# A four-layer graph network on one core: a bias record of full height, another order of work where two graphs meet, and idle products in the ending

## What is computed

```python
# layer 0: convolution over the nodes, messages by distance, a GRU cell
h = relu(bn1(conv1d(x^T, w1, 1 tap)))
x_conv = relu(bn2(conv1d(h, w2, 17 taps)) + x^T)
s = x @ w_se.T + b_se                       # 3 factors per node
dist = sq[:, None] + sq[None, :] - 2 * s @ s.T      # sq = sum(s * s)
x_nmp = (exp(-dist) * mask) @ relu(x @ w_msg.T + b_msg)
r, z = sigmoid(...), sigmoid(...)           # gates of x, x_conv, x_nmp
n = tanh(gi_n + r * gh_n)
x0 = layernorm(x + (1 - z) * n + z * x)
# layer 1: attention on the edges, sigmoid(q @ k.T / sqrt(128)) * adj, normed by degree
# layer 2: logmap0, adj @ x, expmap0, project
# layer 3: adj + I normed by degree, a linear map, relu
```

## Time and profile before

| | |
|---|---|
| Time, median of 3 runs | 765.79 us (764.44 to 767.04) |
| The profiled execution | 766.93 us, span 765.1 us |
| TensorE products busy | 92% of the span |
| VectorE busy | 81% |
| ScalarE busy | 55% |
| GpSimd busy | 17% |
| TensorE's mean granted clock | 0.977 of full |

### The profile page before, as it was taken

One profiled execution on the slowest core, in us unless ns is written; L12 is line 12 of the kernel. 1 busy time (PEld: TensorE's weight loads), 2 busy tenths in 40 slices (PEclk: granted clock), 3 DMA queues, 4 the chain that ended last, 5 costly groups with the idle time before them and its releaser, 6 DMA issues.

```text
span 765.1 us, 12798 instructions
## 1 busy us (share of the span) xinstructions
PE 704.0 (92%) x3968; PEld 544.0 (71%) x3968; DVE 621.8 (81%) x2081; ACT 422.9 (55%) x883; POOL 131.3 (17%) x151
## 2 busy tenths in 40 slices
PE   4879999999999999999999999999999999998653
PEld 3666868777787877777786877778687777775541
DVE  7556788889888888889888888988888888976765
ACT  4353736657384655647374665738465564734351
POOL 0000111212121221212121121212122121211221
PEclk9999999999999999999999999999999999998787
DMA  5306041331605133250604233060513325101000
GB/s 203 124 7 226 17 152 69 124 126 28 220 15 178 55 132 115 77 170 14 211 36 151 82 123 124 23 224 14 178 55 127 120 71 176 56 12 59 0 15 28
DMA packets 46445, 75.26 MB, mean 98 GB/s; under 512 B 4050, under 2 KB 12628, under 8 KB 46292
## 3 DMA queue, kind: packets, MB, share of 16 engines
q1 hardware_dynamic: 46420, 74.96, 29.0%
HBM read 70.76 MB, written 4.19 MB: 98 GB/s over the span
## 4 chain that ended last, share of the span: by engine, by line
PE 62%; DVE 20%; ACT 8%; issue 6%; POOL 4%; DVEq 0%; ACTq 0%; POOLq 0%
PE C L1429 7%; PE F L1437 7%; PE K L1466 7%; PE K L1332 6%; PE F L1359 6%; PE K L1301 5%; PE CONV L1332 4%; PE C L1359 3%; PE C L1301 3%; POOL RSTD L367 3%; ACT X L427 2%; PE K L1320 2%; PE K L1475 2%; DVE X L717 2%; DVE Z L1032 2%
## 5 line engine op out<-in xcount | busy, mean ns | idle before, releaser
L348 POOL TENSOR_TENSOR RSTD<-VEPS,POW 128x4 f32<-128x4 f32 x48 | 49.2, 1024 | 293.1 <-DVE VEPS L711 293.1
L1332 PE MATMUL CONV<-H1H,WH 128*128 128x256 f32 x288 | 83.3, 289 | 2.9 <-DVE H1L L729 2.9
L1332 PE MATMUL CONV<-H1L,WH 128*128 128x256 f32 x288 | 81.9, 284 | 0.0
L1332 PE MATMUL CONV<-H1H,WL 128*128 128x256 f32 x288 | 81.5, 283 | 0.0
L1429 PE MATMUL C<-QT,KT 128*128 128x512 f32 x128 | 60.9, 616 | 4.1 <-DVE KT L869 3.4
L1301 PEld LDWEIGHTS K<-XS,BIG 128*128 128x128 f32 x496 | 59.4, 196 | 3.9 <-DVE XS L998 2.5
L1301 PE MATMUL K<-XS,BIG 128*128 128x128 f32 x496 | 59.8, 280 | 2.5 <-DVE XS L998 2.5
L1437 PE MATMUL F<-A,MSG 128*128 128x512 f32 x128 | 57.6, 593 | 1.1 <-issue 1.1
L1332 PEld LDWEIGHTS CONV<-H1H,WH 128*128 128x128 f32 x288 | 55.3, 192 | 4.5 <-ACT H L436 3.6
L1332 PEld LDWEIGHTS CONV<-H1L,WH 128*128 128x128 f32 x288 | 55.3, 192 | 0.7
L1332 PEld LDWEIGHTS CONV<-H1H,WL 128*128 128x128 f32 x288 | 55.5, 193 | 0.0
(11 more groups left out here) (273 smaller groups left out, 1946.2 us busy)
## 6 DMA issues: line engine op xcount, KB each, us to landing
ADJF<-in_adjT SPq DMA_DIRECT2D x16, 1024.0 KB, 5.3
ADJN<-in_adj SPq DMA_DIRECT2D x16, 1024.0 KB, 7.7
ADJM<-in_adjT SPq DMA_DIRECT2D x15, 1024.0 KB, 5.5
ADJR<-in_adjT SPq DMA_DIRECT2D x14, 1024.0 KB, 5.3
X_IN<-in_xT SPq DMA_DIRECT2D x16, 256.0 KB, 2.6
out<-OUT SPq DMA_DIRECT2D x16, 256.0 KB, 2.8
BIG<-in_weights SPq DMA_DIRECT2D x1, 1088.0 KB, 5.4
BIG<-in_weights SPq DMA_DIRECT2D x1, 576.0 KB, 8.7
```

What stands on the lines that cost most here:

```text
L348: nc.gpsimd.tensor_tensor(RSTD[:, row, :], VEPS[:, row, :], POW[:, 0, :], ALU.pow).then_inc(ev[f"ln{layer}_rstd"], 1)
L1332: last = mm(out, w[:, at_col + k * P:at_col + (k + 1) * P], h[:, k:k + PH], start=(k == 0 and i == 0), stop=(k == count - 1 and i == 2))
```

## The change

It has four parts.

- `SE`, `SEZ`, `SEH` and `ONER` have 128 rows instead of 2; the rows added to `SE` are zero. `factors` makes the bias product last of its four instead of first.
- On ScalarE the two passes of `first_conv` move from the end of a step to the next one, behind its `new_state`; `parts` moves ahead of `update_gate`.
- On VectorE `stacked` is split into its two operations. The left one stands ahead of `new_input`; `kept_state` and `gated` follow it, then the right one, and `rest_of_h1` last. On TensorE step 1 too does the distances ahead of its first taps.
- The ending gets 69 products whose result nobody reads (into bank F1), in five places.

```diff
-        SE = sb("SE", [2, P])
-        SEZ, SEH = sb("SEZ", [2, P], F32R), sb("SEH", [2, P], F32R)
-        ONER = sb("ONER", [2, N], F32R)
+        SE = sb("SE", [P, P])
+        SEZ, SEH = sb("SEZ", [P, P], F32R), sb("SEH", [P, P], F32R)
+        ONER = sb("ONER", [P, N], F32R)
...
                 if mid:
                     new_state(n)
+                    first_conv(n["f"], n["f_prev"])
...
                 if following:
                     squares(n["f_next"])
-                    first_conv(n["f_next"], n["f"])
+                    parts(n["f_next"])
                 update_gate(n)
-                if following:
-                    parts(n["f_next"])
...
                 reset(n)
                 if following:
-                    rest_of_h1(n["f_next"], n["f"])
+                    stacked_left(n["f_next"])
+                new_input(n)
                 if following:
                     kept_state(n["f"])
-                new_input(n)
-                if following:
-                    stacked(n["f_next"])
                     gated(n["f"])
+                    stacked_right(n["f_next"])
+                    rest_of_h1(n["f_next"], n["f"])
...
+            def kept_busy(count):
+
+                for k in range(count):
+                    mm(F1[:, :], WH[:, 0:P], XH[:, :], start=True, stop=True)
+
...
-                mm(K0[:, :], SEH[:, :], ONER[:, :], start=True, stop=False)
                 for k, (w, x) in enumerate(((WH, XH), (WH, XL), (WL, XH))):
-                    last = mm(K0[:, :], w[:, W_SE:W_SE + P], x[:, :], start=False, stop=(k == 2))
+                    mm(K0[:, :], w[:, W_SE:W_SE + P], x[:, :], start=(k == 0), stop=False)
+                last = mm(K0[:, :], SEH[:, :], ONER[:, :], start=False, stop=True)
...
-                starting = isinstance(t, int) and t < 2
+                starting = isinstance(t, int) and t < 1
...
                 last_linear(a)
+                kept_busy(7)
 
                 first_norm_by_features(b)
                 projections(b)
                 attention(b)
+                kept_busy(16)
                 attention_degree(b)
+                kept_busy(8)
                 attended(b)
                 support(b)
+                kept_busy(28)
                 support(c)
                 last_aggregation(b)
                 last_linear(b)
+                kept_busy(10)
```

More of the change, by code:

```diff
@@ L599, in ending @@
                 new_state(a)
+                first_conv(a["f"], a["f_prev"])
                 nc.scalar.preload_act_table_set("natural_log_exp_and_others")
@@ L669, in _ @@
             dve.wait_ge(s_const, 48)
-            V.tensor_scalar(SEZ[:, :], SE[:, :], PAR[0:2, SE_LEFT:SE_LEFT + 1], None, ALU.mult).then_inc(s_se, 1)
+            V.tensor_scalar(SEZ[:, :], SE[:, :], PAR[:, SE_LEFT:SE_LEFT + 1], None, ALU.mult).then_inc(s_se, 1)
             dve.wait_ge(s_se, 1)
@@ L742, in sum_of_h1, with stacked_left @@
                                 ALU.subtract).then_inc(ev["hsl_ready"], 1)
-            def stacked(count):
+            def stacked_left(count):
                 dve.wait_ge(ev["zr_ready"], count)
@@ L747, in stacked, with stacked_right @@
                                        ALU.mult, ALU.subtract)
+            def stacked_right(count):
+                dve.wait_ge(ev["zr_ready"], count)
                 V.scalar_tensor_tensor(STR[:, :], K0[:, :], PAR[:, R_A:R_A + 1], ZR[:, :].bitcast(F32),
@@ L760, in _ @@
             rest_of_h1(1, 0)
-            stacked(1)
+            stacked_left(1)
+            stacked_right(1)
             split(S_ODD, less_odd, 5)
@@ L1621, in packed @@
     par[1, SE_LEFT] = 1
-    se = zeros((2, P), np.float32)
+    se = zeros((P, P), np.float32)
     for at_col in (0, 3, 6, *range(32, 44, 3)):
-        se[:, at_col:at_col + 3] = i["L0_gnn_b_se"]
+        se[0:2, at_col:at_col + 3] = i["L0_gnn_b_se"]
     par[0:9, L_A], par[0:9, R_A] = 1, 2
```

## The result

| | before | after |
|---|---|---|
| median of the runs | 765.53 us (764.44 to 767.04) | 742.09 us (741.7 to 742.9) |
| ratio, 95% interval | | 0.9697 [0.9683, 0.9711] |
| profiled execution, its span | 766.93, 765.1 | 742.9, 741.1 |
| mean granted clock | 0.977 | 0.990 |

What follows compares the result with a forecast made beforehand. One pipeline of 43.76 us steps, TensorE hardly stopping except at seams, then a serial ending at half clock. Seams 16.0, first seam 1.9, start 0.4, ending 7.7: 26.0 us off, forecast 739.8 us, range 737.5 to 749.

Steps and rivals of the forecast that it cites:

- The mechanism of the seam: Between two graphs: full-height bias record gives 0.37 us, new ScalarE and VectorE order 0.77, together 1.14 us per seam.
- Rival 1: At the factors: a change of operands, not the record's height, costs the 0.37 us; 745.6 us; chance 0.09.
- The wait for Y: At the middle seams: TensorE's 0.61 us wait for Y from VectorE disappears, giving 0.77 us each.
- margin of 0.0 us for the statistics: VectorE at the seam: statistics follow the rest of H1, ready at 434.6 us, with about 0.0 us to spare.
- Rival 3: At the seam: a new wait on VectorE's queue replaces Y's; 745.4 us (half lost) or 750.6 (all); chance 0.06.
- Rival 4: ScalarE at the seam: H1 passes after tanh need two table loads of 1.28 us; 768 us; chance 0.02.
- The first seam: Step 1: Y ready near 46.9 instead of 48.9 us, X moving with it; 1.9 us gained, bounds 0.5 to 3.3.
- PE comes out of its taps at about 52.2: TensorE in step 1: taps, now behind the distances, end at about 52.2 us against 54.1 before.
- The start: First factors gain some 0.6 us, the larger SE load costs at most 0.33; net 0.4 us, bounds -0.1 and 0.6.
- The ending: Graph 16's serial chain: idle products in five holes keep TensorE at full clock; 7.7 us gained.
- I take the clock to stay at full: Ending: holes keep at most about 2.2 us idle, clock stays full; first term, transposes to linear products, gives -2.8 us.
- Rival 2: Ending: the clock falls all the same, losing all 7.7 us plus about 1 of overrun; 748.5 us; chance 0.07.

## Why the prediction was right, and where it was off

- **The mechanism of the seam was right, both halves.** The record of full height gives 0.40 us a step (taken: 0.37), shown apart from its place by the short record put last. What the runs show is that the product of two rows and its neighbours are spaced 0.33 to 0.42 us apart, and those of full height 0.234, and that the weight loads of the short product and of the one behind it start late. Rival 1 is out. The rule of the Trainium skill (TensorE: Matmul & The Clock Gate, LDWEIGHTS), that a load of few rows takes the same time as a full one, agrees with the trace (0.18 against 0.19 us), but can't explain the gain: by it nothing is gained. The sentence that the prediction takes from the same page of the Trainium skill (under "The mechanism"), that a load overlaps a product in flight only when the row group differs, is contradicted by the loads of full height, which run beside products of all 128 rows. The same section of the Trainium skill also lets a load go ahead into a background weight buffer, which the prediction left out; the full-height loads would fit that.
- **The wait for Y is gone and no other took its place.** The order alone gives 0.85 us a step, forecast 0.77. The term counted only the start of Y's transposes; a product that has waited also starts its successor later (Y's transposes to the distances: 0.41 us behind a wait, 0.35 without), and the bias gave 0.03 more. So a seam is worth 1.23 instead of 1.14, and the 14 of them 17.2 instead of 16.0. The last seam gave 0.3 more, which the forecast left out since there was no wait in it; the order alone shows it too (39.84 us for that step, before 40.18). The margin of 0.0 us for the statistics held: they carry no bracket. Rival 3 is out. The mixed order (ScalarE old) shows how near such a wait is: its period is 2.06 us above the changed kernel's. Rival 4 is out too: H1's first pass follows the tanh at once (421.30 behind 420.67), and both kernels make 37 table loads.
- **The first seam** gave 1.16 instead of 1.9 us. Y came 2.65 us earlier (48.92 to 46.27), more than the 2.0 forecast, but some of that is the clock of the execution before: in the kernel with the idle products alone, which has the same program up to there, the half clock came behind Y and Y stood at 47.33. The step that failed is "PE comes out of its taps at about 52.2": it was 53.44, since distances and first taps ran at half clock. TensorE stands idle ahead of them for 2.99 us in one piece, where before it was 1.33 there and 2.54 behind the taps, and the half clock moved from before that hole (the factors, now 0.39 us each instead of 0.63) to behind it. Idle products there return 1.5 us in the profile.
- **The start** was forecast at +0.4 and shows -0.49 in the profiled execution. That is mostly this execution's load: in four others with the new order and the same load the first summed messages came at 26.03 to 26.09 us against 26.36 before, +0.3 (with the record alone at 26.31). The 0.33 us allowed for 63 KB fits the 0.29 between the middle values.
- **The ending** gave 5.86 instead of 7.7 us. The failed step is the first term, "I take the clock to stay at full": in the hole that was filled worst (2.51 us with 1.6 us of idle products) the clock fell, and up to the sums that the degree waits for the ending had won 0.97 us instead of 2.8. Four more idle products and two behind the transposes of the messages returned 1.7 us of the missing 1.8 in the profile, and 1.4 in the median. The later terms held: the second block +0.12 for idle products that overran and -0.91 for the degree (forecast +0.35 and -0.95), the attended products -1.96 (forecast -1.95), the support of graph 16 -0.45 (forecast -0.4), the last aggregation -1.69 (forecast -1.95). Rival 2 is thus partly true: at one of five holes in this execution, at two in that of the idle products alone, at none in that of the short record last. Its reading "in the 10 us behind it" is a little short: the idle time of 2.54 us ends at 54.11, 11 us behind the end of the half clock. And since the old ending took 69.8 to 71.1 us with the same program, up to 1.2 of the 5.86 us can be the clock of the execution before.
- **The sum.** 17.2 + 0.3 + 1.2 - 0.5 + 5.9 = 24.1 (24.0 in the span) against 16.0 + 1.9 + 0.4 + 7.7 = 26.0. The seams gave 1.5 us more than forecast, ending, first seam and start 3.5 less; that the total is off by only 2 us is in part luck. 742.09 us lies above the 741.5 that the prediction gives as its own case's bound (its two bounds, added up, give 738.2 to 741.7) and is inside the range because that holds the rivals as well. The version with both holes filled comes to 739.6 us, which is about what the forecast took for granted without filling them.
- **The signs.** Those for the seam came: bias fourth and 0.24 us behind its neighbour, nothing idle before Y's transposes, a period of 42.54 us, no new releaser. Of the signs of being wrong one came too: the clock dropped in the last 60 us, at 681.85, 59 us from the end.

## What to carry to other kernels

A product of two rows between full ones cost 0.40 us more than a full one here; where a short bias record stands in a loop, try it at full height if its load is off the path. Where an engine waits at a seam, lay out both queues with the durations of the trace and move out of the waited chain what has slack behind it, on both engines together: half of such an order was slower than none (44.60 us a step against 43.37). If idle products are to hold the clock, fill the hole whole and also the small ones beside it, since what is left idle may or may not cost half clock behind it.

## What was not expected of the hardware

- The same idle times (0.88 and 0.69 us) left TensorE at full clock in one execution, put it to half from the first projection on in another and from the second on in a third; behind 1.81 and 1.82 us of idle time the last aggregation took 3.67 us in one and 5.37 in the other.
- The two-row product stretches not only its own place but the one behind it: 0.42 us to the next start and 0.35 to the one after, though both of those are of full height; its own weight load and the next one start only with their products. Together the three intervals cost 0.40 us, more than a whole further product of 512 columns (0.234).
- 64 instead of 1 KB in one of the constants' loads moved the first product by 0.2 to 1.1 us from execution to execution, the middle being 0.3; one of the six executions with 1 KB was 0.5 us late as well.
